# Sixteen written-out rounds of attention on TensorE become four written-out ones and twelve in nested loops

## The reference

```python
q, k_t, v_t = heads(hidden @ W_q), heads(text @ W_k), heads(text @ W_v)
probs_t = softmax(q @ k_t^T * scale)                 # per head, 512 x 508
text_out = probs_t @ v_t
qsem = l2norm(probs_t @ text)                        # per head, 512 x 512
sem = qsem @ l2norm(image)^T                         # 4 columns
probs_ip = softmax(q @ k_ip^T * scale + 0.5 * sem) * mask
out = (text_out + probs_ip @ v_ip) @ W_out + b_out + hidden
```

## Time and profile before

| | |
|---|---|
| runs | 1719.3, 1725.77, 1734.9 us; median 1725.77 |
| profiled execution | 1725.77 us; its span from the first to the last instruction 1724.0 us |
| mean granted clock of TensorE | 0.989 of 2.4 GHz |
| busy share of the span | TensorE 97%, VectorE 75%, GpSimd 72%, ScalarE 67% |
| first stage / attention / projection, about | 0 to 298 / 298 to 1603 / 1603 to 1724 us |

### The profile page before, as it was taken

The page is one execution under the profiler, slowest core; times in us unless marked ns, Lnnn a source line. Parts: engine busy times, 40 slices in busy tenths (PEclk is TensorE's granted clock), DMA queues, the critical chain, the costliest instruction groups (busy, mean ns, idle before and its releaser), DMA issues.

```text
span 1724.0 us, 47700 instructions
## 1 busy us (share of the span) xinstructions
PE 1666.1 (97%) x13898; PEld 1042.5 (60%) x13898; DVE 1292.5 (75%) x2982; ACT 1154.5 (67%) x2604; POOL 1238.4 (72%) x1157
## 2 busy tenths in 40 slices
PE   4999998799999999999999999999999999999999
PEld 2776675466666666666666666666666666666455
DVE  6454552588888888788888888788888887887784
ACT  4455554677777777777777777777777777777221
POOL 4232333688888888888888888888888888888220
PEclk9899999799999999999999999999999999999999
DMA  5457657666666556566765665665566656554132
GB/s 200 128 142 189 170 149 171 109 106 109 109 122 108 108 108 128 109 119 109 137 114 102 128 108 108 106 130 108 103 110 137 111 117 111 108 102 84 41 115 91
DMA packets 490766, 205.43 MB, mean 119 GB/s; under 512 B 454296, under 2 KB 480224, under 8 KB 490624
## 3 DMA queue, kind: packets, MB, share of 16 engines
q1 hardware_dynamic: 488528, 201.18, 58.4%
q10 hardware_dynamic: 2096, 2.22, 0.4%
HBM read 68.27 MB, written 34.39 MB: 60 GB/s over the span
## 4 chain that ended last, share of the span: by engine, by line
PE 90%; DVE 3%; issue 3%; DMA 2%; ACT 1%; SPq 1%; POOL 0%; DVEq 0%; ACTq 0%; POOLq 0%
PE bank L1416 32%; PE bank L1417 20%; PE bank L1285 11%; PE bank L1381 8%; PE bank L1390 6%; PE bank L1472 4%; PE bank L1421 3%; PE bank L1415 3%; PE bank L1473 1%; PE bank L1342 1%; DMA reduced<-in_L_xattn_W_v 1%; DMA v_parts<-v_sb 1%; PE bank L1270 0%; PE bank L1457 0%; DVE neg_max L1104 0%
## 5 line engine op out<-in xcount | busy, mean ns | idle before, releaser
L1416 PE MATMUL bank<-u_sb,late 127*128 127x508 f16 x2560 | 944.0, 375 | 0.0
L1417 PE MATMUL bank<-u_sb,late 127*128 127x508 f16 (+3 forms) x2560 | 761.1, 297 | 0.0
L1104 DVE TENSOR_REDUCE neg_max<-bank 128x1 f32<-128x508 f32 x640 | 437.9, 684 | 245.2 <-PE bank L1381 240.9
L611 POOL TENSOR_TENSOR wkv<-probs,wkv 128x508 f16<-128x508 f32 x384 | 432.4, 1126 | 177.8 <-ACT wkv L837 177.8
L1415 PE MATMUL bank<-v_ring,late 127*128 127x41 f16 x2560 | 468.2, 183 | 5.8 <-DVE probs L1113 5.8
L1113 DVE SCALAR_TENSOR_TENSOR probs<-bank,probs 128x508 f32<-128x508 f32 x640 | 432.6, 676 | 7.1 <-PE bank L1417 7.1
L618 POOL TENSOR_TENSOR probs<-probs,wkv 128x508 f32<-128x508 f32 x384 | 428.0, 1114 | 0.0
L1415 PEld LDWEIGHTS bank<-v_ring,late 127*128 127x128 f16 x2560 | 246.4, 96 | 238.3 <-issue 9.6
L1416 PEld LDWEIGHTS bank<-u_sb,late 127*128 127x128 f16 x2560 | 248.0, 97 | 170.5 <-issue 0.9
L625 POOL TENSOR_TENSOR probs<-probs,v_sb 128x508 f32<-128x508 f32 x256 | 295.9, 1156 | 0.0
L817 ACT ACTIVATE exp_bias<-neg_max 128x1 f32<-128x1 f32 x384 | 77.9, 203 | 281.2 <-DVE neg_max L1104 281.2
(11 more groups left out here) (150 smaller groups left out, 1774.2 us busy)
## 6 DMA issues: line engine op xcount, KB each, us to landing
raw<-k_parts SPq DMA_DIRECT2D x192, 79.4 KB, 3.5
raw<-in_ctx_cols SPq DMA_DIRECT2D x8, 1016.0 KB, 7.1
raw<-q_parts SPq DMA_DIRECT2D x32, 240.0 KB, 3.4
u_parts<-u_sb SPq DMA_DIRECT2D x8, 825.5 KB, 9.9
u_sb<-u_parts SPq DMA_DIRECT2D x8, 825.5 KB, 5.4
v_parts<-v_sb SPq DMA_DIRECT2D x8, 820.0 KB, 13.0
v_ring<-v_parts SPq DMA_DIRECT2D x32, 205.0 KB, 4.0
raw<-in_x_cols SPq DMA_DIRECT2D x8, 768.0 KB, 4.3
```

Of the source, the lines that this page charges most:

```text
L611: nc.gpsimd.tensor_tensor(rows[:, 1, :, 0:TP], probs[:, j % PROB_RING, :].rearrange("p (k t) -> p k t", k=TT), rows[:, 0, :, 0:TP], ALU.su ...
L1104: nc.vector.tensor_reduce(neg_max[:, j % 4:j % 4 + 1], bank[S_BANK + j % 2][:, 0:T], AX.X, ALU.max, negate=True)\
L1416: nc.tensor.matmul(y, hi_k, u_sb[0:TP, par, GH[k]:GH[k] + T], start=(k == 0), stop=False)
L1417: done = nc.tensor.matmul(y[:, k * TP:T], hi_k, u_sb[0:TP, par, UL[k]:UL[k] + U_COLS[k]], start=False, stop=(k == TT - 1))
```

## The change

In TensorE's program alone, the Python loop over 16 rounds is replaced. Rounds 0 and 1 (batch 0) and rounds 14 and 15 (batch 7) stay written out. Rounds 2 to 13 are run by a loop of three passes (`pair`); its body holds, for each of the two batches of a pair, the wait for the Gram matrix, one increment of a semaphore that nobody waits for (`apart`), and an inner loop of two passes (`half`) over one round. The round's number is then `4 * pair + 2 + 2 * par + half`, a value in registers, so that every count that a wait in the body tests is computed when the program runs. The half of `u_sb` is still a constant in each body. The order of all matmuls and the numbers tested are as before.

```diff
-            for rnd in range(ROUNDS):
-                if rnd % 2 == 0:
-                    pe.wait_ge(u_loaded, 16 * (rnd // 2 + 1))
-                units(rnd, rnd // 2 % 2, rnd == ROUNDS - 1)
+            pe.wait_ge(u_loaded, 16)
+            units(0, 0, False)
+            units(1, 0, False)
+            with pe.Fori(0, B // 2 - 1) as pair:
+                for par in range(2):
+                    pe.wait_ge(u_loaded, 16 * (2 * pair + par + 2))
+                    apart(pe)
+                    with pe.Fori(0, 2) as half:
+                        units(4 * pair + 2 + 2 * par + half, 1 - par, False)
+            pe.wait_ge(u_loaded, 16 * B)
+            units(ROUNDS - 2, 1, False)
+            units(ROUNDS - 1, 1, True)
```

## The result

The changed kernel takes 1748.5 us (median of 6 runs, 1746.6 to 1753.5) against 1725.5 us before (6 runs, 1718.4 to 1734.9): ratio 1.0163, 95% interval 1.0137 to 1.0188. I had forecast 1737 us (a ratio of about 1.0065). The direction held. The time lies above the range of the case that I forecast (1731 to 1744 us) and inside the range of all cases (1726 to 1755); the difference came out at 23 us where the sum said 11.

What follows compares the result with a forecast made beforehand. TensorE, busy 1273.9 of 1279.7 us in attention, was taken as the bound. Five jump misses × 1.8 = 9 us plus 2 us for waits gave 1735.0 us, 1737 with 1.8 us beyond the span; range 1726 to 1755 us.

Steps and rivals of the forecast that it cites:

- the case that I forecast: TensorE's loop jumps: five misses or about that, plus 2 us for waits; 1737 us, range 1731 to 1744, chance 0.45.
- The bound: Attention: TensorE idles only 5.8 us, and stopping its instruction stream longer than the work queued is paid in full.
- Code volume: TensorE's code packets: twelve rounds stream some 77 written out, about 13 looped; nothing waits for them, so worth 0.
- How many jumps miss: TensorE's eight jumps back: both outer ones and half of the six inner ones miss their code, five misses.
- What a miss costs: Per jump: 3.4 us of stopped issue less 1.4 us of cover and about 0.2 us of swallowed gaps, 1.8 us net.
- Waits against registers: TensorE's 4.4 waits a unit compare with computed counts, mostly computed before the wait is satisfied: 2 us, from 0 to 10.
- All jumps find their code: Rival for TensorE's loops: no jump refetches, only the waits cost, 0 to 5 us; 1726 to 1731 us, chance 0.17.
- All eight miss, or dearer: Rival: all eight TensorE jumps miss or cost more than SyncE's, 18 to 25 us; 1744 to 1751 us, chance 0.24.
- The clock falls: Rival: stops halve TensorE's clock, 10 us each, 50 us for five, 1786 us; chance 0.09 shared with issue-bound.
- Issue becomes the bound: Rival: register steps at waits stretch each looped unit from 1.99 to 2.1 us, 1774 us; chance 0.09 shared with clock.
- Slightly faster: Rival: stops at round starts let VectorE clear its backlog, ending ten gaps of 5.8 us; 1720 us at best, chance 0.05.
- What would show it: Signs: TensorE idle about 2 us at some of eight round starts, 40 to 60 code packets, rounds of 79.9 us, clock 1.00.

Runs made afterwards that it cites:

- the reduction without the race: Kernel before, with VectorE's head reduction (a copy and an addition) written as two tensor_reduce: 1719.0 us, ratio 0.9960.
- the kernel with the inner loops alone: Changed kernel with the outer loop over pairs written out and the six inner loops of two passes kept: 1756.8 us, ratio 1.0166.
- the kernel with the norm's wait last: Changed kernel with TensorE's wait for the norm put behind the other waits of a unit: 1739.0 us, ratio 1.0078.

## Why the prediction was right in sign and half in size

The sum was 9 us for jumps and 2 us for waits. The attention lost 15.7 us to jumps and 12.1 us beside them. The step that failed most is the second term.

**The bound.** Right: TensorE stands at its limit, and what stops its issue for longer than its lead is paid in full. The idle time to be had was in truth a little more than the 5.8 us that I counted: the reduction without the race gained 7.3 us of attention.

**Code volume: worth 0.** Right as far as the traces show: 105 packets became 75, and no time is to be seen for it.

**How many jumps miss.** I said five of eight, the change had two. That step failed by taking half of an unknown as if it were a value; the reason given for it (it depends on where the body begins) is right, as the kernel with the inner loops alone shows, but that gives none, three or six misses of the inner jumps (where both bodies or one or neither find their code), and three is only the middle of them. That the outer two miss was right.

**What a miss costs.** I said 1.8 us, it was 7.9 (7.5 and 8.2 by the rounds). Two of its terms were wrong, a third was about right. The stop: SyncE's 3.35 us is a good price for TensorE's fetch (3.8 us), but here two came in series, because the target lay at a block's end: 7.1 us. The cover: I took 1.4 us, and 7.1 less 6.0 is 1.1, about right. And the clock: half speed for 3.9 and 6.0 us of work afterwards, 1.9 and 3.0 us, which I had only as a rival at 10 us each. The row that I leaned on, the 10.67 us of idle time, gave the sign but no size; the size is in the runs. Two times 7.9 replaces five times 1.8: 15.7 us instead of 9. That the sum isn't further off is luck, since the count was too high and the price too low.

**Waits against registers: 2 us.** It was 12, and this is the larger mistake: the step that failed is that I put at nothing what a later load does to VectorE. My term looked at the sequencer's arithmetic and took it to be done while the wait is pending. It mostly is. What I overlooked is that two waits against constants share an instruction and two against registers don't, so that for an even unit two further steps stand behind the norm, 0.24 us to the load instead of 0.07. And I wrote that VectorE has slack of 10 us a round and nothing is late twice. The average hides that one order of events repeats every 20 units: 0.16 us later at unit 16 makes VectorE's addition at the end of the twenty start behind GpSimd's, 21 times instead of 4, and costs it 1 us. With that addition out of the race the same 0.16 us cost nothing (1274.7 against 1275.8 us). The earlier trace rows already showed gaps of 0.67 us that come back at the same place, and I used them as idle time to be won rather than asking what made them. The two lines of VectorE that would have told it (a median of 230 ns and a mean of 412) I did not look at.

**The rivals.** "All jumps find their code" holds for the six inner jumps and fails at the two outer ones. "All eight miss, or dearer", 1744 to 1751 us, has the measured time in it, but by another mechanism: few jumps, each dearer, and the waits. "The clock falls" was right in kind and too dear by a factor of three to five. "Issue becomes the bound" is refuted by the kernel with the norm's wait last: the same steps, and rounds mostly of 79.8 to 80.0 us. "Slightly faster" is refuted.

**What would show it.** Of the signs that I named, a clock of 0.5 after a stop was to mean "wrong", and came. Small idle times came too, one in twenty units, though not spread over all of them as the sign had it; and the stops stood at two of the eight starts of rounds that I named.

## What to carry to other kernels

Read a jump's price off the trace by asking three things: is the target's code still there, does the target lie just ahead of a block's end, and does the idle time behind it also bring down the clock. For waits, count only the steps behind the one that is satisfied last, and put that one last. And where two engines alternate with a fixed period, look at the longest duration of each short instruction beside its median: a race that it loses in some periods can be lost in nearly all of them after a shift of 0.2 us elsewhere.

## What the runs showed of the hardware

- TensorE's jump back over one body of 1631 instructions (counted in the compiled listing) found its code in 0.21 to 0.24 us in all kernels but one, where it missed in 4.3 to 4.7 us in three of six cases; over two bodies or more it always missed, in 3.4 to 4.8 us.
- A miss with its target one or two instructions ahead of a block's end, by the fitted count, left the array idle for 5.6 to 6.3 us (at the first jump of the change two stops of issue, 3.8 and 3.3 us); eight or 80 instructions of padding made it 2.8 to 3.8 us. The Trainium skill (Runtime: NRT & Kernel Launch, Instruction fetch mechanics) has TensorE's store as 2048 instructions, refilled in blocks of 256; the serial fetches at one place and the single one eight instructions further agree with the blocks, while the same section's remark that the store is only two lines, reckoned there with 32 KiB, doesn't agree with bodies of six blocks that are found again.
- After each of the 19 stops in the attention of these kernels, idle times of 2.8 to 6.3 us, TensorE's granted clock was at 0.50 (1.2 GHz) for 2.9 to 6.0 us of work; the 1.0 us waits in the batch loop leave it at 1.00. With idle times of 2.8 to 3.8 us it fell after the work had begun again, but for one case of 3.0 us, and within the idle time where that was 5.6 us or more.
- A VectorE instruction on two SBUF operands took 230 ns at the median and up to 1.27 us beside a GpSimd addition, 1.21 us beside one that had started 0.04 us earlier; as a reduction along an axis it took 311 to 324 ns throughout.
